# A graph recommender on one core: layers in rounds of 8 tiles with 16 message slots, loops split and aligned

## What is computed

```python
h = emb; acc = emb
for _ in range(2):
    h = segment_sum(adj_val[:, None] * h[adj_col], adj_row, num_segments=N)
    acc = acc + h
graph_item_embs = acc / 3
combined = graph_item_embs[items] + item_features[items]
seq_hidden = take_along_axis(combined, alias_inputs[..., None], axis=1)
...
select = 12 * l2norm(sess_emb)
scores = select @ l2norm(graph_item_embs).T
```

## Time and profile before

| what | value |
|---|---|
| runs (us) | 4863.41, 4881.14, 4880.63; median 4880.63 |
| span of the profiled execution | 4856.4 us, 48622 instructions; 7.0 us under the fastest of the three runs and 24.7 under the slowest, which bounds what its own time adds to its span |
| busy, share of the span | PE 60%, PEld 37%, DVE 62%, ACT 18%, POOL 61% |
| layer 0 | about 759 to 2566 us |
| layer 1 | about 2593 to 4408 us |
| gathers in the layers (L511) | 2 x 1248, 0.94 us each |
| additions (L1071), one-hot matrices (L1026) | 2496 of 0.416 us, 2496 of 0.542 us |

### The profile page before, as it was taken

One profiled execution on the slowest core, in us unless ns is written; L12 is line 12 of the kernel. 1 busy time (PEld: TensorE's weight loads), 2 busy tenths in 40 slices (PEclk: granted clock), 3 DMA queues, 4 the chain that ended last, 5 costly groups with the idle time before them and its releaser, 6 DMA issues.

```text
span 4856.4 us, 48622 instructions
## 1 busy us (share of the span) xinstructions
PE 2921.2 (60%) x9794; PEld 1777.8 (37%) x9794; DVE 3008.1 (62%) x7270; ACT 870.9 (18%) x3004; POOL 2976.7 (61%) x3071
## 2 busy tenths in 40 slices
PE   4998884555555555555554555555555555554788
PEld 2777772322233233223323223332232233322444
DVE  8999984555565556555654555555555555555455
ACT  1999881000000000000000000000000000004443
POOL 1566666666666666666664666666666666664660
PEclk8888886677767767776777777777777677766798
DMA  0000001111111111111114111111111111134273
GB/s 31 3 4 3 3 3 46 45 46 46 45 46 46 46 44 46 46 46 44 46 46 138 46 46 45 45 46 45 44 46 46 46 45 46 46 98 83 43 118 140
DMA packets 140410, 235.69 MB, mean 49 GB/s; under 512 B 56692, under 2 KB 84272, under 8 KB 140144
## 3 DMA queue, kind: packets, MB, share of 16 engines
q0 software_dynamic: 96288, 178.10, 15.8%
q1 hardware_dynamic: 41476, 55.61, 3.4%
q10 hardware_dynamic: 2508, 0.60, 0.1%
HBM read 193.16 MB, written 41.01 MB: 48 GB/s over the span
## 4 chain that ended last, share of the span: by engine, by line
PE 16%; issue 13%; DVE 12%; another core or an unknown queue 8%; DVEq 6%; ACT 1%; DMA 0%; POOL 0%; SPq 0%; ACTq 0%
PE bank L1345 11%; DVE acc L1071 7%; DVE ring L1026 4%; PE bank L1421 2%; DVEq L1067 1%; DVEq L1071 1%; DVEq L1068 1%; PE bank L1449 1%; PE bank L1408 1%; DVEq L1091 1%; DVEq L1061 1%; PE bank L1390 1%; PE bank L1383 1%; PE bank L1400 0%
## 5 line engine op out<-in xcount | busy, mean ns | idle before, releaser
L1345 PE MATMUL bank<-ring 128*128 128x256 f32 x4992 | 1973.7, 524 | 1646.4 <-DVE ring L1026 1093.0
L1345 PEld LDWEIGHTS bank<-ring 128*128 128x128 f32 x4992 | 1077.9, 247 | 2522.3 <-DVE ring L1026 1514.5
L1071 DVE TENSOR_TENSOR acc<-acc,bank 128x256 f32 x2496 | 1037.5, 416 | 1368.3 <-remote 658.8
L511 POOL DMA_INDIRECT ring<-table,cring x1248 | 1177.4, 943 | 663.9 <-issue 352.9
L511 POOL DMA_INDIRECT ring<-in_L_rec_emb,cring x1248 | 1178.2, 944 | 622.7 <-issue 352.9
L1026 DVE TENSOR_SCALAR ring<-bank,mlo,mval 128x256 f32<-128x256 f32 x2496 | 1351.3, 542 | 18.4 <-DMA ring<-table,cring 10.3
L597 ACT COPY mlo<-ring 128x24 f32 (+1 forms) x104 | 22.0, 211 | 3395.5 <-PE bank L1345 2403.2
L581 ACT ACTIVATE big<-big 128x68 f32<-128x68 bf16 x1764 | 558.7, 406 | 1.2 <-issue 0.9
L1282 PE MATMUL bank<-big,ring 128*128 128x136 f32 x2352 | 435.7, 329 | 80.6 <-issue 20.3
L483 POOL DMA_INDIRECT sorted_edges<-moved,block_to x313 | 394.8, 1261 | 101.2 <-issue 101.2
L1282 PEld LDWEIGHTS bank<-big,ring 128*128 128x128 f32 x2352 | 359.4, 220 | 154.8 <-ACT big L581 91.2
(11 more groups left out here) (209 smaller groups left out, 1625.7 us busy)
## 6 DMA issues: line engine op xcount, KB each, us to landing
scores<-stage SPq DMA_DIRECT2D x48, 512.0 KB
ring<-in_L_rec_emb,cring POOLq DMA_INDIRECT x1248
ring<-table,cring POOLq DMA_INDIRECT x1248
table<-big SPq DMA_DIRECT2D x7, 896.0 KB, 9.2
combined<-ring SPq DMA_DIRECT2D x7, 896.0 KB, 7.8
sorted_edges<-moved,block_to POOLq DMA_INDIRECT x313
ring<-combined,sidi POOLq DMA_INDIRECT x200
sorted_edges<-ring SPq DMA_DIRECT2D x1, 1248.0 KB, 4.4
```

The lines of the kernel that those rows point to most:

```text
L511: pool.indirect_dma_start(msg[:, s, :], None, source, bass.IndirectOffsetOnAxis(cring[:, s:s + 1], 0)).then_inc(s_g[s], 16)
L1071: dve.tensor_tensor(acc[:, bass.ds(off, BUCKET)], acc[:, bass.ds(off, BUCKET)], bank[u % PR][:, 0:BUCKET], ALU.add).then_inc(s_acc, 1)
L1345: pe.matmul(bank[u % PR][:, 0:BUCKET], msg[:, h * T + u, :], onehot[:, u % SR, :], start=True, stop=True).then_inc(s_mm, 1)
```

## The change

`T` is 8 where it was 24, so a layer has 156 rounds and the ring has 16 message slots; `PACE`, `AHEAD` and `LEAD` stay. Of the loops on TensorE and VectorE the first goes over rounds 0 to 47 with the side work, rounds 48 and 49 are written out with it, and a second loop goes over the rest without side work ("bare"). Ahead of each of these loops, and of ScalarE's two, an alignment directive pads the instruction stream so that the code that follows begins at a multiple of 256 instructions. Where more than 8 places of padding are needed, they are jumped over. The semaphores of the readout's gathers `s_sq` are now their own, and the decoded codes have their own strip in the ring's memory.

```diff
-    T = 24
+    T = 8
+    BLOCK = 256
+    PAD = 8
...
-    LOOP = 2 * min(NST // 2 - 1, L // 2, NB // 2)
+    WITH = 2 * min(NST // 2 - 1, L // 2, NB // 2)
+    BARE = max(L, NB)
+    assert BARE % 2 == 0 and WITH <= BARE < NST - 2
...
-        m_code = ring[:, at[0] + 2 * T * D - NT:at[0] + 2 * T * D].bitcast(I32)
-        assert 2 * T * D - NT >= T * D
+        m_code = carve(ring, NT, I32)
...
-        s_sq = s_g[0:2 * NG]
+        s_sq = [sem(f"s_sq{u}") for u in range(2 * NG)]
...
+            act.addr_align(BLOCK, 0, PAD)
             with act.Fori(1, NST // 2) as i:
                 for h in range(2):
                     fetch(0, 2 * i + h, h)
...
-            with act.Fori(0, LOOP // 2) as i:
+            act.addr_align(BLOCK, 0, PAD)
+            with act.Fori(0, WITH // 2) as i:
...
-            def round_step(layer, c, it, h, last=False):
+            def round_step(layer, c, it, h, last=False, bare=False):
...
-                    if layer and u == 0:
+                    if layer and u == 0 and not bare:
                         dve.wait_ge(s_ea, c + 2 if not isinstance(c, int) else min(c, NB) + 2)
...
+            def beside(layer, c, h):
+
                 if layer == 0 and not (isinstance(c, int) and c >= L):
                     session_rows(c, v1)
                 if layer == 1 and not (isinstance(c, int) and c >= NB):
...
-                with dve.Fori(0, LOOP // 2) as i:
+                dve.addr_align(BLOCK, 0, PAD)
+                with dve.Fori(0, WITH // 2) as i:
                     for h in range(2):
                         round_step(layer, 2 * i + h, i, h)
-                for c in range(LOOP, NST):
-                    round_step(layer, c, c // 2, c % 2, last=(c == NST - 1))
+                        beside(layer, 2 * i + h, h)
+                for c in range(WITH, BARE):
+                    round_step(layer, c, c // 2, c % 2)
+                    beside(layer, c, c % 2)
+                dve.addr_align(BLOCK, 0, PAD)
+                with dve.Fori(BARE // 2, NST // 2 - 1) as i:
+                    for h in range(2):
+                        round_step(layer, 2 * i + h, i, h, bare=True)
+                for c in range(NST - 2, NST):
+                    round_step(layer, c, c // 2, c % 2, last=(c == NST - 1), bare=True)
...
-                with pe.Fori(1, LOOP // 2) as i:
+                pe.addr_align(BLOCK, 0, PAD)
+                with pe.Fori(1, WITH // 2) as i:
                     for h in range(2):
                         products(layer, 2 * i + h, h)
                         if layer == 1:
                             transpose_embeddings(2 * i + h, h)
-                for c in range(LOOP, NST):
+                for c in range(WITH, BARE):
                     products(layer, c, c % 2)
                     if layer == 1 and c < NB:
                         transpose_embeddings(c, c % 2)
+                pe.addr_align(BLOCK, 0, PAD)
+                with pe.Fori(BARE // 2, NST // 2) as i:
+                    for h in range(2):
+                        products(layer, 2 * i + h, h)
```

More of the change, by code:

```diff
@@ L635, in _ @@
                     fetch(1, 2 * i + h + 2, h)
-            for c in range(LOOP, max(NB, NST - 2)):
+            for c in range(WITH, max(NB, NST - 2)):
                 if c < NB:
@@ L1143, in read_in @@
                     return
-                dve.wait_ge(s_sq[bt % 2 * NG + k], 16 * (NST + min(LG, L - LG * k) * (bt // 2 + 1)))
+                dve.wait_ge(s_sq[bt % 2 * NG + k], 16 * min(LG, L - LG * k) * (bt // 2 + 1))
                 dve.wait_ge(s_v, chain[0])
@@ L1396, in rows_in @@
                 m, w = NG * bt + k, min(LG, L - LG * k)
-                pe.wait_ge(s_sq[bt % 2 * NG + k], 16 * (NST + w * (bt // 2 + 1)))
+                pe.wait_ge(s_sq[bt % 2 * NG + k], 16 * w * (bt // 2 + 1))
                 ge(pe, s_xc, m if bt else m - 1)
```

## The result

The changed kernel takes 4975.85 us in the median of 4 runs (4962.47 to 4980.35), the kernel before 4878.69 us in the same comparison. The ratio is 1.0197, 95% interval 1.016 to 1.0234: 2.0% slower. Two later comparisons gave 1.0198 (1.0136 to 1.0261) and 1.0216 (1.0177 to 1.0255).

A forecast was written before the change was run, and what follows sets the result against it. It took waits as the bound: GpSimd stopping behind VectorE's slow sequencer. Rounds 30, gate 26 and entries 10 sum to +66 us on 4880.6, about 4945 us; own range 4870 to 5020, with rivals 4410 to 5060.

The forecast's parts named there:

- GpSimd stands because TensorE is 12 tiles behind, and TensorE because VectorE is: Before gathers in both layers: GpSimd's 180 stops, 538.6 us, put down to TensorE lagging behind a late VectorE.
- Side work in the first 50 rounds: VectorE's side work, packed denser: a round takes 7.2 us, under GpSimd's 10.0 us, so it stays covered; 0.
- Slow stretches come from the indirect DMAs' traffic: VectorE's sequencer falls to 0.7 us and more for an instruction because of gather traffic, not where instructions stand.
- Smaller bodies, 0: VectorE's loop bodies at a block's beginning, 266 or 256 instructions down to 88 to 106: no gain taken, 0.
- rival (a): VectorE's slow sequencer was instruction supply, and bodies lying in one block end it: 4420 us, chance 0.22.
- Three times the rounds, +30: 156 rounds a layer for 52, each with a load of offsets into registers on VectorE: +30 us, up to +80.
- GpSimd's gate, +26 of 0 to 52: Before every eighth gather, GpSimd now always needs ScalarE's copies too, 0.5 us at 52 more stops a layer: +26 us.
- Stricter gate, 0: GpSimd's gate needs k - 8 products for k - 12: costs 0 where VectorE never runs dry.
- Entries, +10: Entering the padded loops, four of them on VectorE's path at 2.06 us each: +10 us.
- Rival (b): Slow stretches stay but the tighter GpSimd gate cuts them short: about 4680 us, chance 0.13.
- Rival (c): VectorE starts a train 8 tiles behind, not 12, and runs dry: 172 us on top of 66, 5120 us, chance 0.13.

## Why the prediction was right in the number and wrong in the reason

The forecast was 4945 us, with its own range of 4870 to 5020; 4976 is in it. Step by step:

- *GpSimd stands because TensorE is 12 tiles behind, and TensorE because VectorE is.* **This step failed for the kernel before.** It took the named releaser of the earlier trace rows at its word. At 94 of 151 stops the product was there before the train ended, and only 17 stops, 85 of 528 us, end at once with it. GpSimd stops when it meets a gate in a slow stretch, for 3.19 us in the median of these 94, with the product done before the train ended. For the changed kernel's rounds with side work the step holds (44 of 50 stops).
- *Side work in the first 50 rounds: "It stays covered; 0".* **This step failed, and it is the largest term.** The sum compared 7.2 us for a round with GpSimd's 10.0, at the pace of a good stretch, and left out that the same instructions take some 0.7 us each in a slow stretch. Where it is packed into the first 400 tiles of each layer the stops are 91 us longer in sum (261 for 169); the other 1696 tiles have 28 us more. Less the gates' second hop (below) the first part is some 80 us, an estimate.
- *Slow stretches come from the indirect DMAs' traffic.* Half right. Without gathers there are none (a register addition takes 47 ns at most); with half the bytes the stops get longer (a median of 6.7 us for 3.6). The number of the other queues' instructions counts as well, an idle engine's included (with SyncE busy the stretches begin at 7.8 us for 9.2).
- *Smaller bodies, 0.* Right: with bodies of 88 to 106 instructions at the beginning of a block a register addition still takes up to 724 ns, and rival (a) (4420 us) falls with it. What of a body stays loaded, on which that rival was set, no run shows. The padding alone is rather a loss (24 us).
- *Three times the rounds, +30.* The load of 8 offsets takes 598 ns, inside my 0.53 to 0.73. But where the rounds have no side work the stops grow by only 28 us, which the second hop accounts for, so no part of the 30 is seen there. In the rounds with side work it can't be told from the side work: the rounds bring the seams three times as often, and that a seam in a slow stretch is paid in full is my estimate.
- *GpSimd's gate, +26 of 0 to 52.* The mechanism was right and the size too small. Every gate is now two hops, ScalarE's release and then its own. At stops whose product had ended over 5 us before the train, GpSimd stood 3.16 us before (median of 32) and 3.52 us now (of 50). That is 0.4 us at the some 100 gates that did not have the copies, about 40 us, an estimate.
- Not in my sum: stretches that begin sooner (9.2 us for 11.2) and catch gates 8 gathers into a train. They make the 28 short stops, but these stand in the 1696 cheap tiles and cost little by themselves.
- *Stricter gate, 0*: shown alone (0.9972). *Entries, +10*: the padding with them may be up to 24 us; not separated. My own range does not add up as written either: 80, 52 and 10 alone bring 4880.6 to 5023, without the "as much again" that it claims.
- Rival (b), stretches cut short by the tighter gate: no, there is no sign of it, the layers got longer. Rival (c), VectorE runs dry: it does a little more often (85.3 us ahead of the one-hot matrices for 18.4), but the run without padding has 109.4 us of it and is faster, so it is not what costs.

So some 40 + 80 = 120 us of stops stand where I had 66, and the span grew by 104. That the forecast came within 31 us (4976 for 4945) is luck in part: a term of 30 that does not show by itself, a gate too small, and a term at 0 that was the largest.

The side work as the cause is read from the traces, from where the late products are and how they move with the rounds of 16 and vanish with fewer waits. No run took the side work away or spread it over all 156 rounds. That run would settle it, and it is also the obvious next change.

Open: what joins gathers and instructions into one limit. It would have to fit SyncE's share (stretches that begin at 7.8 us for 9.2) and half the bytes in the same 96288 packets (8.5 us for 9.2); no run here shows what it is, and whether the kernel has these stretches without any recording was not tried. Nor were gates at every 16th gather, which by my estimate would meet fewer slow stretches.

## What to carry to other kernels

Before a wait is put down to the engine that the profile names, compare when the awaited instruction ended with when the waiting one moved. Here a gap of several microseconds that ended for all waiting engines at once was not the producer's lateness (GpSimd stood 3.19 us at 94 of 151 stops, the product done before the train ended); such a gate cost by how often it was met in that state and by how many engines hand it on (3.52 us with two hops, 3.16 with one). A gap of nothing was the producer's lateness (58 of the 172 stops of the changed kernel), and a kernel can have both. Count them by stage: here the one kind fills the kernel before and the other the changed kernel's first 400 tiles. And side work that is covered at the good pace has to be covered in the slow stretches too, at 0.7 us for an instruction. Instructions that seem free on an idle queue cost 123 us here beside the trains of gathers. Rounds of 16 for 8 (1.0048 for 1.0197) and half as many waits for products in the changed kernel (58 us less) were worth more here than small aligned loops, whose padding seems to cost 24 us.

## What the runs showed of the hardware

- In trains of gathers (one each 1.25 us) VectorE's sequencer fell from 40 ns to about 0.7 us for an instruction, in the median 8 to 11 us after the restart. SyncE's, where it was given work, fell from 17 ns to 0.7 us; its first such record came 3.5 us after the restart (median). Behind the last gather VectorE's went on for 2.2 us in the kernel before and 2.8 us in the changed one (medians). ScalarE shows it by copies that begin late, 10.1 us after their product before gather 976; its own sequencer records in the layers stay under 0.1 us (65 ns at most). TensorE's take up to 213 ns there in the kernel before and 305 ns in the changed one, GpSimd's 17 ns but for its wait between the layers. Yet where the product was done before the train ended, GpSimd stood 3.19 us in the kernel before (median of 94 stops).
- The stretch started sooner where more instructions ran on the core. The median from a restart to VectorE's first sequencer record of over 0.5 us is 7.8 us with SyncE busy, 9.2 in the changed kernel (9.2 in each of its two repeats) and 11.2 in the kernel before. The number of instructions is not all of it: without padding it is 9.3 and 10.5, with half the rows 8.5.
- A gather of 64 rows makes as many packets as one of 128 (96288 in all), and takes 0.90 us for 0.95 us on GpSimd.
- A load of 8 registers takes 598 ns and one of 24 takes 1600 ns: 75 and 67 ns for a register.
- Loops of 88 to 266 instructions ran with nearly no packets of instructions in the 1400 us from 1000 to 2400 us: 8 in the kernel before, 11 in the changed one, 9 and 10 in the two runs without padding.
